# GpSimd's products with B for two units at once, in a fused bidirectional Mamba and FFN kernel

## The reference

```python
x, z = split(h @ W_in.T)                       # 256 channels each
x   = silu(conv4(x) + conv_b)                  # causal, 4 taps, per channel
dt, Bm, Cm = split(x @ Wx.T)                   # 64, 16, 16
dt  = softplus(dt @ Wdt.T + bdt)
dA  = exp(dt[..., None] * A)                   # 256 channels x 16 states
dBx = (dt * x)[..., None] * Bm[:, :, None, :]
hc  = dA_t * hc + dBx_t                        # the scan over the tokens
y_t = sum_n(hc * C_t)                          # over the 16 states
out = ((y + x * Dp) * silu(z)) @ W_out.T
```

## Time and profile before

| | us |
|---|---|
| median of 3 runs | 936.53 (931.85 to 939.06) |
| the profiled execution | 934.87 |
| its span, first to last instruction | 933.1 |
| DVE busy | 846.0 |
| POOL busy | 844.8 |
| PE busy | 664.9 |
| ACT busy | 586.9 |
| mean granted TensorE clock | 0.824 |

### The profile page before, as it was taken

The page is one execution under the profiler, slowest core; times in us unless marked ns, Lnnn a source line. Parts: engine busy times, 40 slices in busy tenths (PEclk is TensorE's granted clock), DMA queues, the critical chain, the costliest instruction groups (busy, mean ns, idle before and its releaser), DMA issues.

```text
span 933.1 us, 8223 instructions
## 1 busy us (share of the span) xinstructions
PE 664.9 (71%) x2094; PEld 221.7 (24%) x2094; DVE 846.0 (91%) x914; ACT 586.9 (63%) x958; POOL 844.8 (91%) x409
## 2 busy tenths in 40 slices
PE   6758777778677786768678776778678676766663
PEld 3312222213122221213122221223222221112123
DVE  3279999999999999999999999999999999999956
ACT  2556757665776756675676766675677666663524
POOL 0299999998999999999999999999999999999922
PEclk9878897878889887798789788798779789657686
DMA  2785746663665746563675646464575546463003
GB/s 61 161 227 96 177 91 135 144 110 100 132 167 102 167 98 120 130 125 113 115 193 102 130 114 125 131 125 129 106 179 99 101 127 128 135 135 105 23 0 91
DMA packets 46752, 113.12 MB, mean 121 GB/s; under 512 B 7152, under 2 KB 20464, under 8 KB 46576
## 3 DMA queue, kind: packets, MB, share of 16 engines
q1 hardware_dynamic: 46704, 112.59, 54.1%
HBM read 40.48 MB, written 4.98 MB: 49 GB/s over the span
## 4 chain that ended last, share of the span: by engine, by line
DVE 35%; POOL 26%; issue 17%; PE 11%; ACT 9%; DVEq 1%; DMA 0%; SPq 0%; ACTq 0%; POOLq 0%
DVE hs L892 27%; POOL dbx L440 18%; POOL ch L450 7%; DVE ch L808 5%; PE y_ps L1141 3%; PE y_ps L1158 2%; ACT da_ps L654 2%; PE c_ps L1132 2%; ACT L587 1%; PE pre L1087 1%; ACT L589 1%; ACT step L588 1%; ACT hs L725 1%; PE y_ps L1160 1%; DVE gated L819 1%
## 5 line engine op out<-in xcount | busy, mean ns | idle before, releaser
L440 POOL TENSOR_TENSOR dbx<-step_rep,bc_rep 128x1024 f32<-128x1024 f32 x256 | 598.4, 2373 | 12.3 <-DMA step_rep<-step 12.3
L654 ACT ACTIVATE da_ps<-step_rep,neg_a 128x512 f32<-128x512 f32 x512 | 348.2, 687 | 254.8 <-DVE hs L892 249.6
L892 DVE TENSOR_TENSOR_SCAN hs<-da_ps,dbx 128x512 f32<-128x512 f32 x256 | 297.0, 1207 | 33.9 <-ACT da_ps L654 21.6
L892 DVE TENSOR_TENSOR_SCAN hs<-da_ps,carry,dbx 128x512 f32<-128x512 f32 x256 | 312.4, 1269 | 11.3 <-ACT da_ps L654 11.3
L1141 PE MATMUL y_ps<-ch,stack 128*32 128x512 f32 x1024 | 172.5, 750 | 160.9 <-DVE ch L808 108.4
L808 DVE TENSOR_TENSOR ch<-hs,c_ps 128x1024 f32<-128x1024 f32 x176 | 210.7, 1197 | 0.1
L450 POOL TENSOR_TENSOR ch<-hs,bc_rep 128x1024 f32<-128x1024 f32 x80 | 189.5, 2368 | 14.6 <-DVE hs L892 9.0
L1132 PE MATMUL c_ps<-x_dbl,select 128*128 128x512 f32 x256 | 186.5, 819 | 0.0
L1087 PE MATMUL pre<-h_t,w_conv 128*128 128x512 f32 x256 | 123.2, 626 | 9.2 <-ACT xs L560 8.5
L1141 PEld LDWEIGHTS y_ps<-ch,stack 128*32 128x32 f32 x1024 | 23.9, 117 | 263.3 <-issue 169.2
L1132 PEld LDWEIGHTS c_ps<-x_dbl,select 128*128 128x128 f32 x256 | 48.1, 234 | 140.9 <-issue 130.0
(11 more groups left out here) (157 smaller groups left out, 453.6 us busy)
## 6 DMA issues: line engine op xcount, KB each, us to landing
step_rep<-step SPq DMA_DIRECT2D x128, 512.0 KB, 8.3
bc_rep<-bc_rows SPq DMA_DIRECT2D x64, 512.0 KB, 5.8
h_in<-in_L_attn_hidden_states SPq DMA_DIRECT2D x4, 512.0 KB, 8.7
h_res<-in_L_attn_hidden_states SPq DMA_DIRECT2D x4, 512.0 KB, 9.0
x_rows<-xn SPq DMA_DIRECT2D x7, 256.0 KB, 7.7
bc_rep<-x_rows SPq DMA_DIRECT2D x1, 1536.0 KB, 12.0
out<-hs SPq DMA_DIRECT2D x3, 512.0 KB, 3.2
bc_rows<-x_dbl SPq DMA_DIRECT2D x16, 64.0 KB
```

The source lines that it names most:

```text
L440: nc.gpsimd.tensor_tensor(dbx[:, n % RING], dtx_rep[:, r], b_rep[:, s % 2, k, :].unsqueeze(1).to_broadcast([P, 2, CHUNK]), ALU.mult).then_ ...
L654: nc.scalar.activation(da_ps[:, half % DA_BANKS, :], dt_rep[:, r, e, :], ACT.Exp, scale=neg_a[:, half_of(unit), 2 * (unit % 2) + e, g, k:k ...
L892: nc.vector.tensor_tensor_scan(in_scan_order(hs[:, n % RING, e, :], s), in_scan_order(da_ps[:, (2 * n + e) % DA_BANKS, :], s), in_scan_ord ...
```

## The change

It has three parts. **On POOL**, the B products of units n and n+1 (n even) become one instruction of 2048 columns (`times_b_pair`), which is issued at the even step n-2. It waits until unit n-3 has been scanned and counts `dbx_ready` up by 2 when it ends. Only the first two units of the whole kernel are still made one at a time. **On DVE**, where both units of an even and odd pair have their C product on DVE (`joined`: units 2 and 3, 6 and 7, and 14 and 15, or 12 and 13 in group 3), one instruction of 2048 columns makes both, after the scan that follows the second (`times_c_pair`). **In the prologue** the first loads are cut in pieces and reordered, ten transposes without a use run first on TensorE, the second convolution gets a PSUM bank of its own, dt and dt x are made for each half of the channels apart (the first half's dt x on DVE), and the first `step_rep` loads stand ahead of three of the four `bc_rep` loads.

```diff
 EXPS_AHEAD = 1
-B_AHEAD = 3
 DA_BANKS = 3
...
+def joined(s, n):
+
+    return n not in POOL_C[s] and n ^ 1 not in POOL_C[s]
...
-            sp.dma_start(h_in[:], h_tiles[0]).then_inc(h_in_ready, 16)
-            sp.dma_start(w_in_raw, w_in.rearrange("(q p) m -> p q m", p=P)).then_inc(w_in_in, 16)
...
+            sp.dma_start(w_in_raw[:, 0:DT, :], w_in_quarters[:, 0:DT, :]).then_inc(w_in_in, 16)
+            sp.dma_start(h_in[:, 0:TT, :], h_tiles[0][:, 0:TT, :]).then_inc(h_first_in, 16)
+            sp.dma_start(h_in[:, TT:2 * TT, :], h_tiles[0][:, TT:2 * TT, :]).then_inc(h_in_ready, 16)
...
-                sp.wait_ge(dtx_ready, group + 1)
+                if group == 0 and r < 2:
+                    sp.wait_ge(first_dtx, 1)
+                else:
+                    sp.wait_ge(dtx_ready, group + 1)
...
             load_bc(0, 0, 0)
-            load_bc(0, 0, 1)
             load_step(0, 0, 0)
             load_step(0, 0, 1)
-            for k in range(2, STATES // QUAD):
+            for k in range(1, STATES // QUAD):
                 load_bc(0, 0, k)
...
+            def times_b_pair(b, s, n):
+
+                group, r, k = NG * b + s, slot_of(n), quad_of(n)
+                if k == 0:
+                    pool.wait_ge(step_in[r], 2 * 16 * (group + 1))
+                    pool.wait_ge(step_in[r + 1], 2 * 16 * (group + 1))
+                if half_of(n) == 0:
+                    pool.wait_ge(bc_in[s % 2][k], 16 * (group // 2 + 1))
+                if not (group == 0 and n < RING):
+
+                    pool.wait_ge(scanned, 2 * (UNITS * group + n - RING + 2))
+                nc.gpsimd.tensor_tensor(dbx[:, n % RING:n % RING + 2].rearrange("p u e t -> p (u e) t"),
+                                        dtx_rep[:, r:r + 2].rearrange("p u e t -> p (u e) t"),
+                                        b_rep[:, s % 2, k, :].unsqueeze(1).to_broadcast([P, 4, CHUNK]),
+                                        ALU.mult).then_inc(dbx_ready, 2)
...
-                        if n + B_AHEAD < UNITS:
-                            times_b(b, s, n + B_AHEAD)
-                        elif not (last and s == NG - 1):
-                            times_b(*following(b, s), n + B_AHEAD - UNITS)
+                        if n % 2 == 0 and n + 2 < UNITS:
+                            times_b_pair(b, s, n + 2)
+                        elif n % 2 == 0 and not (last and s == NG - 1):
+                            times_b_pair(*following(b, s), 0)
...
-            times_step(0, 0)
-            for n in range(B_AHEAD):
+            pool.wait_ge(dt_ready, 1)
+            pool.wait_ge(xs_ready, 1)
+            nc.gpsimd.tensor_tensor(step[:, 1, 1, :], step[:, 1, 0, :], xs[:, 0, 1, :], ALU.mult).then_inc(dtx_ready, 1)
+            for n in range(2):
                 times_b(0, 0, n)
...
-            nc.scalar.preload_act_table_set(EXP)
-            act.wait_ge(dt_cols_in, 16 * 6)
-            for stage in LATER_STAGES:
-                prepare(0, 0, stage)
...
+            nc.scalar.activation(step[:, 0, 0, :], u[:, 0], ACT.Softplus).then_inc(first_dt, 1)
+            prepare(0, 0, "take u1")
+            act.wait_ge(u_taken, 2)
+            nc.scalar.activation(step[:, 1, 0, :], u[:, 1], ACT.Softplus).then_inc(dt_ready, 1)
...
+                dve.wait_ge(first_dt, 1)
+                dve.wait_ge(xs_ready, 1)
+                nc.vector.tensor_tensor(step[:, 0, 1, :], step[:, 0, 0, :], xs[:, 0, 0, :], ALU.mult).then_inc(first_dtx, 1)
...
+            def times_c_pair(b, s, n):
+
+                group = NG * b + s
+                dve.wait_ge(c_ps_ready, (UNITS * group + n) // 2 + 1)
+                dve.wait_ge(scanned, 2 * (UNITS * group + n + 2))
+                if not (group == 0 and n < RING):
+                    dve.wait_ge(summed, UNITS * group + n - RING + 2)
+                nc.vector.tensor_tensor(ch[:, n % RING:n % RING + 2].rearrange("p u e t -> p (u e) t"),
+                                        hs[:, n % RING:n % RING + 2].rearrange("p u e t -> p (u e) t"),
+                                        c_ps[:, n // 2 % C_BANKS, :].unsqueeze(1).to_broadcast([P, 4, CHUNK]),
+                                        ALU.mult).then_inc(ch_vector, 2)
...
-                            if prev[2] not in POOL_C[prev[1]]:
+                            if joined(*prev[1:]):
+                                if prev[2] % 2:
+                                    times_c_pair(prev[0], prev[1], prev[2] - 1)
+                            elif prev[2] not in POOL_C[prev[1]]:
                                 times_c(*prev)
...
+                elif q:
+                    pe.wait_ge(conv_sb, DT * q + 1)
                 else:
-                    pe.wait_ge(conv_sb, DT * q + 1)
+                    bank = c_ps[:, 0, :]
...
-                pe.wait_ge(weights_in, 16 * 9)
+                pe.wait_ge(weights_in, 16 * 10)
...
+            warm_up(10)
             transpose_h(0, 0)
-            transpose_h(0, 1)
             transpose_scaled(FWD, 0)
             transpose_scaled(FWD, 1)
-            transpose_w_z()
             convolve(0, 0, 0, (pads_ready, 2))
+            transpose_h(0, 1)
             convolve(0, 0, 1, None)
             transpose_weights()
-            pe.wait_ge(weights_sb, 4)
             pe.wait_ge(select_ready, 3)
-            make_x_dbl(0, 0, (weights_sb, 4))
+            make_x_dbl(0, 0, (weights_sb, 1))
```

More of the change, by code:

```diff
@@ L213, in build @@
              "z_raw silu_z_ready scaled_ready w_conv_ps w_conv_sb conv_ps conv_sb xs_ready x_dbl_ps x_dbl_sb "
-             "u_ps u_taken dt_ready dtx_ready "
+             "u_ps u_taken dt_ready dtx_ready first_dt first_dtx conv_b_in h_first_in "
              "rows_stored dbx_ready da_ready scanned carried c_ps_ready ch_vector "
@@ L559, in prepare @@
                         act.wait_ge(dtx_ready, q - 1)
-                    nc.scalar.activation(xs[:, par, a, :], pre[:], ACT.Identity, bias=conv_b[:, g, a:a + 1]).then_inc(conv_sb, 1)
+                    bank = c_ps[:, 0, :] if zero and a else pre[:]
+                    nc.scalar.activation(xs[:, par, a, :], bank, ACT.Identity, bias=conv_b[:, g, a:a + 1]).then_inc(conv_sb, 1)
                 if stage == "silu":
@@ L692, in _ @@
             copy_w_conv(FWD, 0)
+            act.wait_ge(conv_b_in, 16)
+            prepare(0, 0, "take conv0")
             copy_ht(0, 1)
-            act.wait_ge(conv_in, 16 * 2)
-            prepare(0, 0, "take conv0")
             prepare(0, 0, "take conv1")
             prepare(0, 0, "silu")
+            nc.scalar.preload_act_table_set(SOFTPLUS)
+            act.wait_ge(dt_cols_in, 16 * 6)
+            prepare(0, 0, "copy x_dbl")
+            prepare(0, 0, "take u0")
+            act.wait_ge(u_taken, 1)
+            nc.scalar.activation(step[:, 0, 0, :], u[:, 0], ACT.Softplus).then_inc(first_dt, 1)
+            prepare(0, 0, "take u1")
+            act.wait_ge(u_taken, 2)
+            nc.scalar.activation(step[:, 1, 0, :], u[:, 1], ACT.Softplus).then_inc(dt_ready, 1)
             nc.scalar.preload_act_table_set(EXP)
-            act.wait_ge(dt_cols_in, 16 * 6)
-            for stage in LATER_STAGES:
-                prepare(0, 0, stage)
             act.wait_ge(a_log_ready, 1)
@@ L758, in _ @@
             dve.wait_ge(w_in_in, 16)
-            dve.wait_ge(conv_in, 16 * 2)
+            dve.wait_ge(conv_in, 16)
             scale_w_in(FWD)
@@ L1019, in transpose_scaled @@
                 ins.then_inc(w_conv_ps, 1)
-            def transpose_w_z():
-                pe.wait_ge(ht_sb, 2)
-                for q in range(DT):
-                    ins = nc.tensor.transpose(c_ps[:, 0, q * P:(q + 1) * P], w_in_raw[:, DT + q, :], ident[:])
-                ins.then_inc(weights_ps, 1)
             def transpose_weights():
-                pe.wait_ge(weights_in, 16 * 9)
+                pe.wait_ge(weights_in, 16 * 10)
                 pe.wait_ge(raw_zero, 1)
@@ L1039, in transpose_weights @@
                 ins.then_inc(weights_ps, 1)
-                pe.wait_ge(conv_sb, 2)
                 for a in range(DT):
-                    ins = nc.tensor.transpose(pre[:, a * P:(a + 1) * P], wx_raw[:, 1, a * P:(a + 1) * P], ident[:])
+                    nc.tensor.transpose(da_ps[:, 1, a * P:(a + 1) * P], wx_raw[:, 1, a * P:(a + 1) * P], ident[:])
+                for a in range(DT):
+                    ins = nc.tensor.transpose(da_ps[:, 1, (DT + a) * P:(DT + a + 1) * P], w_in_raw[:, DT + a, :], ident[:])
                 ins.then_inc(weights_ps, 1)
@@ L1048, in transpose_h @@
             def transpose_h(b, c):
+                if c == 0 and isinstance(b, int) and b == 0:
+                    pe.wait_ge(h_first_in, 16)
+                elif c == 0 or (isinstance(b, int) and b == 0):
+                    pe.wait_ge(h_in_ready, 16 * (b + 1))
                 if c == 0:
-                    pe.wait_ge(h_in_ready, 16 * (b + 1))
                     if not (isinstance(b, int) and b == 0):
@@ L1078, in convolve @@
                 q = NG * b + s
```

(22 more changed lines are left out.)

25 lines of the change are left out of this document (13 added, 12 removed).

## The result

| | before | changed |
|---|---|---|
| median of 4 runs each, us | 934.58 | 952.49 |
| lowest to highest | 931.85 to 939.06 | 952.41 to 953.40 |
| span of the profiled execution | 933.1 | 950.7 |

The recorded ratio is 1.0178, with a 95% interval of 1.0144 to 1.0213: the change costs 1.8%. (The two medians of this table alone would give 1.0192, which is inside that interval.) The forecast was 952.

A forecast was written before the change was run, and what follows sets the result against it. The prediction took POOL to bound the kernel, with DVE close behind. From 934.87 us it added 22.1 for the steady part and took off 5 for the prologue: 952 us, with 940 to 966 holding 8 in 10.

The forecast's parts named there:

- The bound: Steady part before the change: POOL's work, 209.4 us of a 212.6 us batch, sets the pace; DVE has 9 us slack.
- The price of a pair: POOL's 2048-column B product: 4.49 us in a row, range 4.40 to 4.63, against 2.316 for a single one.
- the rival built on it: POOL's B pairs save nothing, 4.63 us each: batch 221.3 us, total 962.5 us; chance 17%.
- The wait: POOL idles in front of C1 until scan 1 ends, 2.52 us in the walked group; 12.1 us idle a batch in all.
- The walk: Hand-timed steps of POOL and DVE through each group, without ACT: 204.9 us of POOL's work plus 12.1 idle a batch.
- The batch: Steady part, four groups: 217.0 us walked, 218.5 with other waits, 5.9 more than before; +22.1 us over 3.75 batches.
- the half that I added: 1.5 us a batch, half of the 3 us missing from the old order's walk, for ACT's late `da_ps` and POOL's old waits.
- C pairs on DVE: Twelve pairs a batch, 2.18 us each, save 0.5 us on DVE, worth nothing; their place costs, included in the walk.
- The 1.07 us in 15 groups: C product work moved between scans 0 and 1, ahead of C1; without it the idle at C1 would be about 1.5.
- The start: New prologue: -5 us, ends -2 and -7; unit 2's scan 3.9 earlier, or 7 with the larger head start.
- ACT's chain to the first `da_ps`: Prologue: it moves earlier by the same 2 to 3 us as x_dbl and doesn't bind.
- the expected waits of DVE: Steady part: DVE waits for `dbx` at units 0, 4 and 14 in place of `da_ps`, which before took 32.9 us.

The follow-up runs named there:

- run 7: Changed kernel with six slots of dbx in place of four, buffers shared for room, each B pair issued four units ahead: 921.4 us, ratio to before 0.9856.
- Runs 4: Changed kernel with each B pair written as two single products at the same place, same waits in front: 932.2 us, ratio to before 0.9965.
- run 5: Changed kernel with unit 14 in place of 13 among POOL's C products in groups 0 to 2, too: 942.1 us, ratio to before 1.0084.
- Run 9: Changed kernel without ScalarE's table switches in the steady part, so values differ: 949.1 us, ratio to before 1.0145.
- run 3: Changed kernel with DVE's C products single again, B pairs and prologue kept: 942.4 us, ratio to before 1.0075.
- run 2: Changed kernel with B products single again, three units ahead, C pairs and prologue kept: 924.3 us, ratio to before 0.9876.

## Why the prediction was right

**The bound.** POOL sets the pace with DVE just behind it: walks made of nothing but these two engines' work and waits come within 1.7% of the batch in all kernels with four slots for which one was made. With six slots POOL's work alone, 204.9, is 2% short of the batch (run 7); there ScalarE's delays are no longer covered by POOL.

**The price of a pair.** Forecast 4.49 us in a row. In the changed kernel's timeline two pairs in a row, from the start of the first to the start of what follows, give it: 320.38 to 329.34 is 2 x 4.48. The price that was worked out from the smallest norm instruction was the true one; twice a single one, 4.63, and the rival built on it are out. The Trainium skill's 4497 ns ("GPSIMD Engine Reference", section 3.1 Elementwise) stands beside a busy time of 4533 ns here, 0.8% more.

**The wait.** The walk had 2.78 us of idle in front of C1 in a group with a carry; the row says 2.75. It had 12.1 us a batch in all, 45 to 48 us; the rows say 41.4 and 9.0, 50.4 us, of which 35.3 are in front of C1 in 15 groups. DVE was to wait for `dbx` at units 0, 4 and 14, and it does, 34 times, as the table in the section on the result shows. Runs 4, 5 and 7 lessen POOL's wait in three ways, by the moment at which the first product counts, by what stands in the hole, and by more slots: from 50.2 us between 60 and 870 us to 9.0, 35.9 and 10.1. They give back 20, 10 and 31 us.

**The batch.** 217.0 walked, 1.5 added for ScalarE and other old waits, 218.5 measured. Run 9's batch is 1.1 lower, which would make most of the 1.5 ScalarE's; it is one execution against one, and the times don't resolve it. That the half that I added was the right half is partly luck: the other runs with four slots stand 1.2 to 2.9 us over their walks.

**C pairs on DVE.** Their price was right (313.30 to 315.48 is 2.18), and that they cost by their place, only beside B pairs, too: 10 us of 952 (run 3), nothing beside single ones (run 2). The 1.07 us in 15 groups would be 16; a third of that didn't show. The place in front of scan 1 isn't the whole of it: in run 5 no C pair stands there, and they cost 15.7.

**The start.** -5 forecast, -5.6 measured at unit 2; the number was right, but two of its steps weren't. x_dbl came 3.6 us earlier (its store is issued at 20.43, where it was 24.01), and not 2 to 3; the step loads 7.1 earlier, not 6. The prediction had the pair (2, 3) start when the sixth load lands, at 46.15 - 2.7 = 43.4. The sixth load, now one of `bc_rep`, landed at 40.8 and held nothing back. What held the pair back was unit 1's product in front of it, which waits for the fifth load: 39.44 + 2.30 = 41.74, and 4.49 + 0.13 behind it is 46.36. And ACT's chain to the first `da_ps`, which was not to bind, does: the first scan starts at 37.79, right behind its `da_ps`, 5.3 us earlier than before and not 6.8, as POOL's product alone would allow. That costs nothing further on, since unit 1 waits for its product. The written steps came to -3.9 at unit 2, and -5 was a choice between that and -7: this is luck in part.

**The sum.** 952 is also helped by two misses that cancel. The start gave 7.0 us by the start of dt x in group 0, 2 more than forecast. The rest cost 24.6 and not 22.1: the next two groups lost 5.8 us, where two groups at the steady rate lose 2.9, and the end lost 1.0.

**What was wrong.** Beside the steps of the start, the expected waits of DVE were one-sided: ScalarE's were to give way to POOL's, and about half of them, 17.5 of 32.9 us, stayed. They are at other units, 15 and 10 above all. The walk, which knows no ScalarE, has DVE wait 2.33 us for the pair (0, 1) behind a group without a carry; the trace has 0.9 there (groups 3, 7 and 11), behind 1.2 at unit 15 for `da_ps`. Run 9 shows the exchange: ScalarE's wait is gone there, and the one for the pair is 2.2. This is why so little of ScalarE's delay shows in the time. No part of the sum rested on it but the 1.5 us a batch.
